# Spreading delta in float32 by pairs of 32-row products, with four decay banks, in a Mamba + MoE kernel

## What is computed

```python
delta = jnp.einsum('blr,dr->bdl', dt, dt_proj_w) + dt_proj_b[None, :, None]
delta = jax.nn.softplus(delta)
A = -jnp.exp(A_log)
deltaA = jnp.exp(jnp.einsum('bdl,dn->bdln', delta, A))       # d = 256 inner channels, n = 16 states
deltaB_u = jnp.einsum('bdl,bnl,bdl->bdln', delta, Bm, uc)
def step(state, inp):
    dA, dBu, Ct = inp
    state = dA * state + dBu
    y = jnp.einsum('bdn,bn->bd', state, Ct)
    return (state, y)
...
y = (y + uc * D[None, :, None]) * _silu(z)
out = jnp.einsum('bdl,ed->ble', y, out_proj_w)               # + x, layer norm, then the experts
```

## Time and profile before

| | us |
|---|---|
| median of 3 runs | 922.57 (919.72 to 924.37) |
| the profiled execution's own time | 926.12 |
| its span, from the first to the last instruction | 924.2 |
| first scan starts | 71.00 |
| last scan ends | 651.3 |

### The profile page before, as it was taken

The page is one execution under the profiler, slowest core; times in us unless marked ns, Lnnn a source line. Parts: engine busy times, 40 slices in busy tenths (PEclk is TensorE's granted clock), DMA queues, the critical chain, the costliest instruction groups (busy, mean ns, idle before and its releaser), DMA issues. The chain is left out here.

```text
span 924.2 us, 11664 instructions
## 1 busy us (share of the span) xinstructions
PE 606.1 (66%) x2666; PEld 294.8 (32%) x2666; DVE 650.0 (70%) x998; ACT 447.8 (48%) x908; POOL 612.5 (66%) x628
## 2 busy tenths in 40 slices
PE   4766757768767777675875755756417889888700
PEld 2221111312222232131232121221207778777700
DVE  2037888989998998998998899999432333333353
ACT  3536656474654746736557444334103444444323
POOL 5024476585797797797978789877753655556544
PEclk8775687776686686697577665565556999999955
DMA  3057438376666876657557646862015666666463
GB/s 79 0 126 175 99 91 194 92 170 137 140 165 158 226 166 144 142 135 177 116 132 160 143 113 160 193 147 68 30 60 143 185 172 180 173 177 188 122 183 89
DMA packets 76338, 128.22 MB, mean 139 GB/s; under 512 B 10544, under 2 KB 53488, under 8 KB 68080
## 3 DMA queue, kind: packets, MB, share of 16 engines
q1 hardware_dynamic: 71920, 118.43, 53.0%
q0 software_dynamic: 4352, 9.05, 3.2%
HBM read 102.64 MB, written 18.51 MB: 131 GB/s over the span
## 5 line engine op out<-in xcount | busy, mean ns | idle before, releaser
L517 POOL TENSOR_TENSOR hc<-hs,Crep 128x1024 f32<-128x1024 f32 x128 | 308.3, 2409 | 116.6 <-DVE hs L1263 91.0
L1263 DVE TENSOR_TENSOR_SCAN hs<-bank,state,flow 128x512 f32<-128x512 f32 x256 | 314.7, 1269 | 42.4 <-ACT bank L1033 36.4
L1033 ACT ACTIVATE bank<-bank,negA 128x512 f32<-128x512 f32 x256 | 167.0, 660 | 175.2 <-PE bank L740 171.5
L740 PE MATMUL bank<-dparts,sel 96*128 96x512 bf16 x256 | 128.7, 512 | 134.9 <-DVE hs L1263 127.8
L1253 DVE TENSOR_TENSOR flow<-flow,bank 128x2048 f32<-128x2048 f32 x64 | 145.2, 2269 | 13.7 <-issue 12.3
L740 PEld LDWEIGHTS bank<-dparts,sel 96*128 96x128 bf16 x256 | 27.5, 109 | 315.0 <-DVE hs L1263 263.2
L1185 ACT ACTIVATE flow<-bank,b1T 128x128 f32<-128x128 f32 x288 | 82.2, 369 | 88.7 <-PE bank L914 77.2
L749 PE MATMUL bank<-hc,kc 128*32 128x512 f32 x512 | 98.9, 856 | 18.3 <-DVE yg L1271 14.7
L914 PE MATMUL bank<-flow 128*128 128x128 f32 x576 | 82.9, 288 | 23.4 <-issue 15.2
L639 POOL DMA_INDIRECT results<-flow,idn x72 | 72.2, 1003 | 33.8 <-issue 32.0
L698 PE MATMUL bank<-hT,wtapT 128*128 128x512 f32 x128 | 77.0, 742 | 14.6 <-ACT hT L969 10.8
(11 more groups left out here) (168 smaller groups left out, 806.1 us busy)
## 6 DMA issues: line engine op xcount, KB each, us to landing
flow<-du_d SPq DMA_DIRECT2D x64, 1024.0 KB
flow<-L_ffn_W SPq DMA_DIRECT2D x72, 256.0 KB
dparts<-part SPq DMA_DIRECT2D x96, 64.0 KB
xg<-xs SPq DMA_DIRECT2D x72, 66.0 KB, 2.6
du_d<-du SPq DMA_DIRECT2D x32, 128.0 KB, 2.3
hs<-results SPq DMA_DIRECT2D x16, 256.0 KB, 3.5
xin<-L_attn_x SPq DMA_DIRECT2D x8, 256.0 KB, 3.0
spill<-xn SPq DMA_DIRECT2D x8, 256.0 KB
```

The costliest lines, as they stand in the source:

```text
L517: nc.gpsimd.tensor_tensor(hc[:, Q % 2, two, :], hs[:, Q % 2, two, :], Crep[u % 2][:].unsqueeze(1).broadcast_to([P, 2, T]), ALU.mult).then_ ...
L740: nc.tensor.matmul(dbank[G % 3][:], sel[:, g // 4 % 4, :], dparts[u % 2][:, 4 * (g // 16) + g % 4, :])\
L1033: nc.scalar.activation(dbank[G % 3][:], dbank[G % 3][:], ACT.Exp, scale=negA[:, ch:ch + 1]).then_inc(s_ex, 1)
L1263: nc.vector.tensor_tensor_scan(hs[:, Q % 2, j, :], dbank[G % 3][:], flow[Q % 3][:, j, :], state[:, Q // QUADS % 2, Q % QUADS, j:j + 1], AL ...
```

## The change

- **Delta stays float32.** `spread_pair` replaces `spread_delta`: for two steps at once, two float32 products of 32 rows each, on the partitions 32i to 32i+31 where the delta of tile i already lies, with `sel` in float32 on 128 partitions. The parts (two casts on ACT, two subtractions on POOL) and the 96 DMAs `stack` are gone.
- **Four decay banks** (bank0 to bank3). A pair of spreads waits for the second scan of the pair before the last one.
- **Softplus** is regrouped: POOL adds relu and exp(-|x|) (`relu_plus_exp`), ACT makes -(1+e) and its logarithm, DVE does two `scalar_tensor_tensor` (`add_log`, after step 14) instead of three operations (after step 11), and `delta_u` follows after step 15 instead of 17. `delta` gets two buffers.
- **The back's products** go through the front's two banks (now bank6 and bank7), in the order of a longer table `FILLS`; `drained` counts by which engine a bank is emptied.
- `Crep` has three buffers. The taps of the convolution are spread over single steps. The SiLU stands after step 26 instead of 24, and u1 and z0 are emptied at step 24.
- `one_hots` compares with the integer indices, without the cast.
- **The head** works unit 0's SiLU, softplus and delta*u by halves of the channels, stores and spreads the first half first, in four DMAs for the first quad, and leaves the second half of unit 1's convolution and its z to the steps 2 to 4 of unit 0.

```diff
-FILLS = ("T", "u0", "u1", "z0", "z1", "x", "c", "dt0", "dt1")
-FIRST_FILLS = ("T", "u0", "u1", "x", "dt0", "dt1", "c", "z0", "z1")
+def fill_order():
+    order = [(w, 0) for w in ("T", "u0", "u1", "x", "dt0", "dt1", "c")] + [(w, 1) for w in ("T", "u0", "u1", "z0", "z1")]
+    order += [(w, 1) for w in ("x", "dt0", "dt1", "c")] + [(w, 2) for w in ("T", "u0", "u1", "z0", "z1", "x")]
+    for j in range(1, UNITS):
+        late, early = j + 1 < UNITS, j + 2 < UNITS
+        order += [(w, j + 1) for w in ("dt0", "dt1", "c") if late]
+        order += [("ranks", j - 2)] if j >= 2 else []
+        order += [(w, j + 2) for w in ("T", "u0") if early]
+        order += [("out", j - 1)]
+        order += [(w, j + 2) for w in ("u1", "z0", "z1") if early]
+        order += [("xn", j - 1), ("logits", j - 1)]
+        order += [("x", j + 2)] if early else []
+    last = UNITS - 1
+    return order + [("ranks", last - 1), ("out", last), ("xn", last), ("logits", last), ("ranks", last)]
...
-        dbank, Brep, ybank, fbank, mbank = bank[0:3], bank[3], bank[4], bank[5:7], bank[7]
+        dbank, Brep, ybank, fbank = bank[0:4], bank[4], bank[5], bank[6:8]
...
-        Crep = [sb(f"Crep{b}", [P, T]) for b in range(B)]
-        delta = sb("delta", [P, HALVES, T])
+        Crep = [sb(f"Crep{r}", [P, T]) for r in range(3)]
+        delta = [sb(f"delta{b}", [P, HALVES, T]) for b in range(2)]
...
+                if u == 0 and q < 4:
+                    sp.wait_ge(s_duw0, 64)
+                else:
+                    sp.wait_ge(s_duw[u % 2], 64 * (u // 2 + 1))
...
+            def spread_first_du():
+                sp.wait_ge(s_duw0, 64)
+                for j in range(4):
+                    sp.dma_start(flow[0][:, j, :], du_d[0, 0, 0, :, T * j:T * j + T].unsqueeze(0).broadcast_to([N, CH, T]))\
+                        .then_inc(s_dul0[j], 16)
...
+            def relu_plus_exp(u):
+                pool.wait_ge(s_e, u + 2)
+                drained(pool, fill_of(u, "dt1"))
+                nc.gpsimd.tensor_tensor(relu[:], relu[:], rest[:], ALU.add).then_inc(s_rl, 1)
...
-                add_at, rest_at, low_at = (6, 8, 10) if j else (8, 10, 12)
...
+                    if slot == (4 if j else 8) and late:
+                        relu_plus_exp(j + 1)
...
+                        if slot in (6, 7, 8, 9):
+                            list_rows(j - 2, 0, slot - 6)
...
-            def spread_delta(G):
-                u, g = G // STEPS, G % STEPS
-                if g == 0:
-                    pe.wait_ge(s_dst[u % 2], 192 * (u // 2 + 1))
-                after(pe, s_sc, G - 2)
-                nc.tensor.matmul(dbank[G % 3][:], sel[:, g // 4 % 4, :], dparts[u % 2][:, 4 * (g // 16) + g % 4, :])\
-                    .then_inc(s_dr, 1)
+            def spread_pair(R):
+                u, r = R // (STEPS // 2), R % (STEPS // 2)
+                if R == 0:
+                    pe.wait_ge(s_silu, 1)
+                if r in (0, 8):
+                    pe.wait_ge(s_dl, 2 * u + (1 if r == 0 else 2))
+                after(pe, s_sc, 2 * R - 2)
+                q, j = r // 2, 2 * (r % 2)
+                for i in (j, j + 1):
+                    ins = nc.tensor.matmul(dbank[i][:], sel[32 * i:32 * i + 32, q % 4, :],
+                                           delta[u % 2][32 * i:32 * i + 32, q // 4, :])
+                ins.then_inc(s_dr, 1)
...
                 for g in range(STEPS):
-                    spread_delta(STEPS * j + g)
+                    if g % 2 == 0:
+                        spread_pair((STEPS * j + g) // 2)
...
+                    if late:
+                        if g == 1:
+                            proj_dt(j + 1, 0)
+                        if g == 3:
+                            proj_dt(j + 1, 1)
+                        if g == 4:
+                            spread_c(j + 1)
+                    if g == 5 and j >= 2:
+                        ranks(j - 2)
+                    if early:
+                        if g == 7:
+                            xhat_T(j + 2)
+                        if g in (9, 11, 12, 13):
+                            conv_u(j + 2, 0, ((9, 11, 12, 13).index(g),))
+                    if g == 15:
+                        add_skip(j, 0)
+                    if g == 16:
+                        out_proj(j - 1, (0, 1))
+                    if g == 17:
+                        out_proj(j - 1, (2, 3))
+                    if early:
+                        if g in (19, 20, 21, 23):
+                            conv_u(j + 2, 1, ((19, 20, 21, 23).index(g),))
+                        if g == 24:
+                            proj_z(j + 2, 0)
+                        if g == 25:
+                            proj_z(j + 2, 1)
+                    if g == 27:
+                        xn_T(j - 1)
+                    if g == 29:
+                        logits(j - 1)
+                    if early:
+                        if g == 29:
+                            proj_x(j + 2, (0,))
+                        if g == 31:
+                            proj_x(j + 2, (1,))
...
             def first_host(g):
+                if g == 2:
+                    conv_u(1, 1, every)
                 if g == 3:
+                    proj_z(1, 0)
+                if g == 4:
+                    proj_z(1, 1)
+                if g == 7:
...
+            def first_silus():
+                for h in range(HALVES):
+                    o = filled(0, ("u0", "u1")[h])
+                    nc.scalar.activation(uc[0][:, h, :], o[:], ACT.Silu, bias=cb[:, h:h + 1]).then_inc(s_fd, 1)
+                for h in range(HALVES):
+                    act.wait_ge(s_z0, h + 1)
+                    ins = nc.scalar.activation(sz[0][:, h, :], dbank[h][:], ACT.Silu)
+                ins.then_inc(s_silu, 1)
...
+                nc.scalar.activation(minus_w[:], rest[:], ACT.Copy, bias=-1.0, scale=-1.0).then_inc(s_1pe, 1)
...
+                act.wait_ge(s_1pe, u)
+                after(act, s_dr, STEPS // 2 * (u - 1))
+                nc.scalar.activation(delta[u % 2][:], minus_w[:], ACT.Ln, scale=-1.0).then_inc(s_ln, 1)
...
                     if late:
                         if g == 1:
+                            abs_relu(j + 1, 0)
+                        if g == 3:
+                            abs_relu(j + 1, 1)
+                        if g == 4:
+                            exponential(j + 1)
+                        if g == 5:
+                            one_plus(j + 1)
                             c_evac(j + 1)
-                        if g == 2:
-                            abs_relu(j + 1, 0)
-                        if g == 4:
-                            abs_relu(j + 1, 1)
-                        if g == 5:
-                            exponential(j + 1)
-                        if g == 6:
-                            one_plus(j + 1)
                         if g == 8:
                             logarithm(j + 1)
-                        if g == 16:
-                            hi_part(j + 1)
-                        if g == 20:
-                            mid_part(j + 1)
                     if early:
+                        if g == 2:
+                            xhats(j + 2)
                         if g == 7:
-                            xhats(j + 2)
-                        if g == 10:
                             h_evac(j + 2)
                         if g == 14:
                             u_evac(j + 2, 0)
-                        if g == 18:
+                        if g == 24:
                             u_evac(j + 2, 1)
-                        if g == 21:
                             z_evac(j + 2, 0)
-                        if g == 22:
+                        if g == 25:
                             z_evac(j + 2, 1)
-                        if g == 24:
+                        if g == 26:
                             silus(j + 2)
-                        if g == 29:
+                        if g == 31:
                             xdbl_evac(j + 2)
...
+            def add_log(u):
+                dve.wait_ge(s_ln, u)
+                nc.vector.scalar_tensor_tensor(delta[u % 2][:], minus_w[:], 1.0, delta[u % 2][:], ALU.add, ALU.add)\
+                    .then_inc(s_bend, 1)
+                dve.wait_ge(s_bend, u)
+                dve.wait_ge(s_rl, u + 1)
+                nc.vector.scalar_tensor_tensor(delta[u % 2][:], delta[u % 2][:], 0.0, relu[:], ALU.min, ALU.add)\
+                    .then_inc(s_dl, 2)
...
+            def first_delta():
+                for h in range(HALVES):
+                    d = delta[0][:, h, :]
+                    dve.wait_ge(s_ln0, h + 1)
+                    nc.vector.scalar_tensor_tensor(d, minus_w[:, h, :], 1.0, d, ALU.add, ALU.add).then_inc(s_bend0, 1)
+                    dve.wait_ge(s_bend0, h + 1)
+                    dve.wait_ge(s_rl, 1)
+                    nc.vector.scalar_tensor_tensor(d, d, 0.0, relu[:, h, :], ALU.min, ALU.add).then_inc(s_dl, 1)
```

(9 more changed lines are left out.)

468 lines of the change are left out of this document (205 added, 263 removed).

## The result

The changed kernel takes 954.44 us (median of 4 runs, 950.47 to 958.99) against 921.46 for the kernel before (4 runs, 919.72 to 924.37). The ratio is 1.0356, with a 95% interval of 1.0295 to 1.0417. (The table ahead of the prediction has 922.57, from the first three of the four runs before.) I had forecast 886, faster. The profiled execution took 950.47, with a span of 948.7.

What follows compares the result with a forecast made beforehand. It took VectorE's (DVE's) in-order list in the scans, its work plus 42.4 us of waiting, as the bound; -14 -21 -8.5 -1 +8 = -36.5 off the 922.57 median gave 886 us, range 867 to 912.

Steps and rivals of the forecast that it cites:

- Head, minus 14: Before the first scan: earlier SiLU, delta*u and spread bring that scan from 71.00 to 57, 14 us less.
- Pairs: On PE: two 32-row float32 spreads run beside each other, 1.06 us at full clock and 1.94 at half clock.
- one after the other: Rival, on PE: the two spreads of a pair run serially, 1.9 us at full clock, giving 912; chance 0.10.
- the two rivals about PE: Pairs run serially, 912, chance 0.10; or PE at half clock becomes the bound, 952, chance 0.07.
- Logarithm, minus 8.5: On DVE in the scan stage: one of three operations of 1.22 us goes, seven times, 8.5 us less.
- collision, plus 8: On DVE after step 14: the logarithm's first operation waits 1.2 to 1.3 us for POOL's product, 8 us more.
- The cast's going: On DVE, ahead of the one-hot comparison: dropping the cast saves 0.15 us a unit, 1 us in all.
- Waiting, minus 21: DVE's waits ahead of scans: four decay banks and a later SiLU cut 36.2 us to 15.4, 21 less.
- Hidden: ACT, POOL, DMAs and the two shared banks: nothing there is waited for except through the other terms; no size.
- Step 3, whose wait was to go: In the middle units, DVE's 0.2 us wait at the scan of step 3 goes with the third `Crep`.
- PE at half clock: Rival, slower: in six units PE's 41 us a unit become 82 and bound the kernel, 952; chance 0.07.

Runs made afterwards that it cites:

- the ninth kernel: Changed kernel with POOL's statistics first, gating at step 7, logarithm behind scan 15, three moves for waits left, four in unit 0: 900.41 us, ratio 0.9725.
- the run with Identity: Against the ninth kernel, the SiLU of units 2 to 7 replaced by Identity: 892.85 us, ratio 0.9665 to the kernel before.
- the last run: Against the ninth kernel, the gating of the unit's first half behind scan 23 instead of 24: 890.13 us, ratio 0.9648 to the kernel before.

## Why the prediction was wrong

- **Head, minus 14: right, in part by luck.** 71.0 to 56.8; I had 57. But the terms that I listed add up to 10.8 to 12.8, not 14. And the spread of delta*u is issued 3 us earlier than I had it (47.18 against 50), while its four parts take 9.6 us until the last of them is multiplied (I had 7), so two errors cancel. Besides, the first scan of the runs with this same head lies anywhere from 55.6 to 58.7.
- **Pairs: right.** Two spreads side by side take 1.13 at full and 2.08 at half clock (rows of unit 4 above), against 1.06 and 1.94 forecast and 1.9 and 3.7 for one after the other. The mean clock did not fall, so the two rivals about PE did not come about. A change between 128-row products and 32-row pairs costs a little. A tap of the kernel before, whose neighbours are full products as well, is followed by the next product 0.86 us after its start at full clock and 1.71 at half clock (medians). The taps above, which have a pair or a sum ahead of them and a pair behind, are followed after 1.02 (403.23 to 404.25) and 2.00 (412.06 to 414.06). That is some 0.1 us a change at full clock and 0.15 at half clock, and, as an estimate, 3 to 5 us of PE a unit for the 32 changes of 16 pairs. The forecast's 1.06, taken from column groups, had as much in it unnoticed. The Trainium skill (TensorEngine Tiling (Array Packing), Key Properties) states that changing the tiling mode drains TensorE. The trace agrees, and the drain is short.
- **Logarithm, minus 8.5, and collision, plus 8: right, the second a little small.** Before, the three operations took 27.6 us in the stage, 2.0 of it collision. Now two take 28.7, 17.0 by themselves and 11.7 collision, so plus 9.7. In the units 1 to 5 the first operation waits 1.45 us, in unit 0 POOL slips in between, both as described; in unit 6 both are held up. The cast's going gave some 5 rather than 1: `oh` and `taken` behind it take 8.5 us in the stage, against 14 with the cast (8.5 for it, and 0.59 and 0.19 for each of the two behind it), because POOL's product is met in only some of the units. Which ones is a matter of luck: in the ninth kernel the same two take 10.7.
- **Waiting, minus 21: wrong, and this alone decided.** It came to plus 42. The failed step is the one headed "Hidden", where I wrote that I "followed the list" for the shared banks and that nothing of ACT's and POOL's is waited for except through the terms named. I had followed the two banks and the releases of the decay banks, but not the other semaphores of the steps that move. `xhats` moved from step 7 to step 2 on ACT while its producer on POOL stayed; `post` moved from step 7 to step 9 on VectorE while its consumer on PE, the sum of step 10, stayed. The rows of the first were to be had: POOL's product and the statistics behind it start only after scan 1 of the same unit, and the move puts their reader in front of decay 3. The moves cost 23 and 16 us here and 25 and 19 in the kernel before. Together they are worth 39, more than the whole sum of 36.5, and they stand in it at nothing.
- **The rest of that term: too hopeful by some 28 us.** With both handoffs mended, idle is 49.2, where the forecast meant 21.4. Unit 0 waits 16 instead of 7. Step 3, whose wait was to go, waits 8 us in four units, the rest of the first handoff. In the middle units the SiLU with its loads was given a cover of 9 us against 8 at full clock, and I had written that at half clock "the wait is back". It was back, in most units (up to 3.5 at step 27, 1.07 at step 30), and I took 1.2 a unit. What step 30 waits for is PE's pair, not the table loads, as the trace of the run with Identity shows. I had the condition and chose its favourable side, at a mean clock of 0.69.
- **Chances.** Slower had 0.07, all for PE at half clock, and its price, 952, lies 2 us from what was measured. That is luck: the clock did not fall, and PE stood idle for 71.4 us ahead of the spreads, waiting for scans (its row above). No rival was a misplaced handoff, though a change that renumbers steps in five engines' lists has many. (A reading was off by one as well: unit 0 has nine waits behind its first scan before, not ten; their sum of 12.6 is right.)

## What to carry over

When an order written by hand is renumbered, take each step that moves, list every semaphore that it waits for and every one that it signals, and look where the other end stands in its own engine's list now. A step that moved ahead of its producer, or behind its consumer, stops an in-order engine with everything queued behind it, decays and spreads above all. A step that frees a shared bank should stand at the first place where its data are there, not where its engine has room: moving a gating by two steps was worth 16 us in one kernel and 19 in the other. And read a gain from the waits that the move was made for: in the last run the time fell by what was forecast, and most of it came from an operation that by chance no longer met POOL's product.
